# A recommender tower on one core: SBUF laid out anew, with TensorE's operands first and on multiples of 512 bytes

## The reference, cut to what matters

```python
def _cin_layer(X0, Xi, W, b):
    H = W.shape[0]
    F0_, Fi = (X0.shape[1], Xi.shape[1])
    Wr = W.reshape(H, F0_, Fi)
    return jnp.einsum('hjk,bjd,bkd->bhd', Wr, X0, Xi) + b[None, :, None]
...
e = jnp.stack([tbl_0[ids[:, 0]], ..., tbl_38[ids[:, 38]]], axis=1)   # 512 x 39 x 16
for W, b in Ws:                                                       # 3 layers, H = 128
    Xi = _cin_layer(X0, Xi, W, b)
    res.append(Xi.sum(axis=2))
...
h = jnp.concatenate([z, dense_ctx], axis=1)                           # 384 + 16
h = jnp.maximum(h @ W_top1 + b_top1, 0.0)                             # 512
h = jnp.maximum(h @ W_top2 + b_top2, 0.0)                             # 256
y = h @ W_top3                                                        # 1
```

## Time and profile before

| | us |
|---|---|
| median of 3 runs | 668.32 (667.62 to 669.49) |
| the profiled execution, its own time | 667.98 |
| its span, first to last instruction | 666.2 |
| TensorE busy | 644.0 |
| ScalarE, VectorE, GpSimd busy | 480.6, 457.2, 497.3 |

### The profile page before, as it was taken

How to read it: one execution, slowest core, us unless ns; L and a number is a source line. 1 busy time by engine, 2 the same in 40 slices (tenths; PEclk the granted TensorE clock), 3 DMA queues, 4 the chain that set the end, 5 groups by cost and what they waited for, 6 DMA issues and landing times.

```text
span 666.2 us, 11234 instructions
## 1 busy us (share of the span) xinstructions
PE 644.0 (97%) x2676; PEld 478.7 (72%) x2676; DVE 457.2 (69%) x1183; ACT 480.6 (72%) x1737; POOL 497.3 (75%) x467
## 2 busy tenths in 40 slices
PE   3599999999999999999999999999999999999998
PEld 1387677777777777777787777777777777779873
DVE  1467777778686968777725786868687777774820
ACT  1457678878787969697834787878796978784912
POOL 5888888979797988888844797979888885553620
PEclk9989999999999999999999999999999999999999
DMA  6643515151514234142400514132241404002000
GB/s 160 143 107 71 125 25 118 36 121 13 140 15 98 58 68 86 38 115 36 119 11 2 119 13 113 20 78 55 47 85 17 115 10 118 4 4 90 5 1 1
DMA packets 68263, 43.32 MB, mean 65 GB/s; under 512 B 49482, under 2 KB 61709, under 8 KB 66457
## 3 DMA queue, kind: packets, MB, share of 16 engines
q1 hardware_dynamic: 56870, 38.04, 25.1%
q0 software_dynamic: 5184, 1.29, 2.3%
q10 hardware_dynamic: 6158, 3.45, 2.0%
HBM read 39.58 MB, written 1.96 MB: 62 GB/s over the span
## 4 chain that ended last, share of the span: by engine, by line
PE 94%; DMA 3%; SPq 1%; DVE 1%; ACT 1%; issue 1%; POOL 0%; ACTq 0%
PE a_ps L704 40%; PE d_ps L704 25%; PE quad_ps L655 14%; PE g_ps L745 5%; PE quad_ps L758 5%; PE a_ps L871 1%; PE quad_ps L672 1%; DMA rows<-x_first 1%; DMA emb<-tables_dram,rows 1%; PE quad_ps L659 1%; PE d_ps L842 1%; DMA x_first<-emb 1%; DMA picks_sb<-picks_dram 1%; PE rows_ps L842 0%; PE a_ps L842 0%
## 5 line engine op out<-in xcount | busy, mean ns | idle before, releaser
L930 ACT ACTIVATE parts<-a_ps,xt 128x128 f32<-128x128 f32 x1536 | 424.2, 383 | 104.5 <-PE a_ps L704 101.2
L551 DVE SCALAR_TENSOR_TENSOR parts<-d_ps,xt,parts 128x128 f32<-128x128 f32 x704 | 201.8, 343 | 108.2 <-PE d_ps L704 107.8
L311 POOL TENSOR_TENSOR parts<-parts 128x512 f32<-128x512 f32 x128 | 163.8, 1297 | 97.8 <-ACT parts L930 97.0
L704 PE MATMUL a_ps<-w_hi,x_hi 128*128 128x512 f32 x384 | 181.5, 473 | 0.6 <-issue 0.6
L311 POOL TENSOR_TENSOR left<-parts 128x512 f32<-128x512 f32 x128 | 166.8, 1319 | 6.5 <-ACT parts L930 4.9
L285 POOL DMA_INDIRECT emb<-tables_dram,rows_now x150 | 144.6, 964 | 25.2 <-issue 17.9
L704 PE MATMUL a_ps<-w_hi,x_lo 128*128 128x512 f32 x384 | 152.3, 397 | 0.6 <-DVE x_lo L520 0.6
L704 PE MATMUL a_ps<-w_lo,x_hi 128*128 128x512 f32 x384 | 151.5, 395 | 0.0
L704 PE MATMUL d_ps<-w_hi,x_hi 128*128 128x512 f32 (+1 forms) x256 | 127.1, 496 | 0.0
L655 PE MATMUL quad_ps<-products,w_sb 117*128 117x512 f32 (+1 forms) x210 | 107.3, 591 | 0.0
L704 PE MATMUL d_ps<-w_lo,x_hi 128*128 128x512 f32 (+1 forms) x256 | 97.7, 382 | 0.6 <-ACT xt L908 0.6
(11 more groups left out here) (72 smaller groups left out, 426.1 us busy)
## 6 DMA issues: line engine op xcount, KB each, us to landing
shifted<-x_rows SPq DMA_DIRECT2D x45, 312.0 KB
shifted<-x_rows SPq DMA_DIRECT2D x45, 234.0 KB
diag<-xt SPq DMA_DIRECT2D x240, 4.9 KB
rows<-x_rows SPq DMA_DIRECT2D x45, 78.0 KB
emb<-tables_dram,rows_now POOLq DMA_INDIRECT x150, 3.2
w_sb<-w_dram SPq DMA_DIRECT2D x6, 384.0 KB
shifted<-x_first SPq DMA_DIRECT2D x12, 136.5 KB
g_sb<-w_dram ACTq DMA_DIRECT2D x2, 768.0 KB, 9.4
```

The lines of the kernel that those rows point to most:

```text
L311: nc.gpsimd.tensor_tensor(to, parts[:, i % 2, now:now + GF, :], parts[:, i % 2, more:more + GF, :], ALU.add).then_inc(pool_added, 1)
L551: nc.vector.scalar_tensor_tensor(now, d_ps[d % D_RING][:, H * at:H * (at + 1)], xt[:, u, i, j:j + 1], before, ALU.mult, ALU.add).then_inc( ...
L704: return nc.tensor.matmul(bank[:, 0:H * len(fields)], x[:, u, 128 * i:128 * (i + 1)], w[:, fields[0]:fields[-1] + 1, :].rearrange("p j h - ...
L930: last = nc.scalar.activation(parts[:, i % 2, 2 + GF * a + at, :], a_ps[(NA * i + a) % A_RING][:, H * at:H * (at + 1)], ACT.Copy, scale=xt ...
```

## The change

Eleven tensors move to the front of SBUF, behind a new one, `spare`, that nothing uses: `w1_hi`, `w1_lo`, `x1_hi`, `x1_lo`, `w0_sb`, `products`, `w2_sb`, `g_sb`, `x2t`, `diag` and `z`. No size, shape or type changes, and on all five engines the same instructions stand in the same order with the same waits; line numbers below the edit are 3 higher.

```diff
@@ -155,6 +155,20 @@
+        spare = sb("spare", [128, 96])
+        w1_hi = sb("w1_hi", [128, FIELDS, H], F32R)
+        w1_lo = sb("w1_lo", [128, FIELDS, H], F32R)
+        x1_hi = sb("x1_hi", [128, 2, CW], F32R)
+        x1_lo = sb("x1_lo", [128, 2, CW], F32R)
+        w0_sb = sb("w0_sb", [PK, QT, H])
+        products = sb("products", [128, QT, CW])
+        w2_sb = sb("w2_sb", [128, FIELDS, H])
+        g_sb = sb("g_sb", [128, FIELDS, HB])
+        x2t = sb("x2t", [128, 2, H])
+        diag = sb("diag", [128, BLKS, BLK_B, FIELDS + 1])
+        z = sb("z", [128, 3, B])
+
         picks0_sb, picks_sb = sb("picks0_sb", [128, PICKS0], I32), sb("picks_sb", [128, PICKS], I32)
@@ -165,10 +179,6 @@
-        w0_sb = sb("w0_sb", [PK, QT, H])
-        w1_hi = sb("w1_hi", [128, FIELDS, H], F32R)
-        w1_lo = sb("w1_lo", [128, FIELDS, H], F32R)
-        w2_sb = sb("w2_sb", [128, FIELDS, H])
         bias_sb = sb("bias_sb", [128, 3])
@@ -182,18 +192,11 @@
         rows3 = sb("rows3", [PK, CW])
-        products = sb("products", [128, QT, CW])
-        x1_hi = sb("x1_hi", [128, 2, CW], F32R)
-        x1_lo = sb("x1_lo", [128, 2, CW], F32R)
...
-        x2t = sb("x2t", [128, 2, H])
-
-        diag = sb("diag", [128, BLKS, BLK_B, FIELDS + 1])
-        g_sb = sb("g_sb", [128, FIELDS, HB])
-        z = sb("z", [128, 3, B])
```

## The result

The changed kernel takes 663.51 us (median of 6 runs, 661.84 to 664.97) against 668.04 us (6 runs, 666.76 to 669.49). The ratio is 0.9938, with a 95% interval from 0.9924 to 0.9953: 4.5 us or 0.6% faster.

What follows compares the result with a forecast made beforehand. TensorE, busy 644.0 of 666.2 us, was taken to bound the kernel. Every term of the change was taken at 0, so the forecast was no change (666.3 to 670.3 us counted as same), with a range of 661 to 672 us.

Steps and rivals of the forecast that it cites:

- What bounds the kernel: Whole kernel: TensorE, busy 644.0 of 666.2 us, sets the time; other engines wait for it, with about 100 us cushion each.
- The sum of 434.5 us for layer 1: Layer-1 matmuls: 1728 at 0.232 us plus 192 at 0.175 us, meeting the chain's 433 us.
- 1 ns a matmul is 1.9 us: Layer-1 matmuls, all 1920: each ns more per matmul was priced at 1.9 us, 0.3% of the time.
- Moving operands of layer 1: Layer-1 `w1` stream, remainder 64 to 0: taken at 0, bounds -9.6 to +15.4 us.
- The irregular intervals: Layer-1 loop: matmul intervals vary from 0.227 to 0.24 us though nobody waits; the prediction could not say by what.
- B: Rival, layer-1 stream: irregularity goes, intervals settle at 0.227 us, 9.6 us less, 658.7 us; chance 0.12.
- 2 to 6 us: Layer-1 stream: the partial gain called as likely as the full 9.6 us of B.
- Rival A: Layer-1 stream: 19 ns excess is misaligned 512-byte reads; freed, 0.2145 us a matmul, 32.7 us less, 635.6 us; chance 0.05.
- Rival C: Layer-1 matmuls: `w1` stream and `x1` weight load, run in step, collide; +15.4 us, 683.7 us, half as likely; chance 0.09.
- fp32 operands and weight loads at 0: TensorE's fp32 passes (0.429 us) and weight loads (188 to 191 ns): new remainders cost 0; passes at most 2.1 us.
- DMA and the start: First 34 us, `emb0` write and read back into `rows3`: taken at 0, bounds +-1.9 us.
- same: Whole kernel: time within 666.3 to 670.3 us, not told from no change; chance 0.74.

Runs made afterwards that it cites:

- the mixed small kernel: TensorE alone on zeros, repeating one fp32 matmul, then six or nine float32r ones; with nine, 2947 ns all at 0, 2951 to 2954 mostly at difference 128.

## Why the prediction was right or wrong

**What bounds the kernel: right.** The time followed TensorE's own instructions; the other engines moved by about a microsecond. The sum of 434.5 us for layer 1 was right too, and so was "1 ns a matmul is 1.9 us", as an upper bound. One part was not: engines behind TensorE were held to be covered by about 100 us of idle time each. That is a sum over the program. With TensorE 0.36 us a chunk faster, VectorE came late at one place in each of 12 chunks and took 1.0 us back. The prediction listed the waits of TensorE's matmuls and not those of its weight loads, where this bank already stood:

```profile
PEld d_ps L704 <- DVE parts L551: 8.7, 39, 0.2
```

**Moving operands of layer 1, taken at 0: wrong, and the failed step is the comparison.** The term measured 3.4 ns for each matmul of 512 columns. The prediction set `w1` at remainder 64 against `ctx_split` at 448 and found the same 1.10 us. Two things were wrong with it. It compared remainders of the moving operand, where the pair of operands counts: `ctx_split` and its stationary partner in `x1_lo` both start at 448, difference 0, the good case, and `w1` over `x1` is difference 128, the bad one. And it read a lone float32r matmul behind fp32 passes, in which the good case does not show: in the mixed small kernel the interval at that place is 630 to 639 ns at difference 0 and 631 to 638 at 128. A row that does not stand in a run of its own kind cannot price the run.

**The irregular intervals: the right trace, not followed.** The prediction saw 0.227 to 0.24 in a loop where nobody waits and wrote "I can't say by what". Those were the effect. It priced the end of it rightly, 0.227 for each, and overstated the total (9.6 us for B) by taking all 1920; the mean fell by 3.4 ns, not 5, and 1.0 us came back as waits. The measured 4.5 us lie in the "2 to 6 us" that the prediction named as equally likely, without a working of its own; that the result fell inside the stated range is owed to this rider and not to the term of 0.

**Rival A (the full 19 ns as a misaligned read): wrong.** Its 0.2145 us never appears. 226.7 is the lowest settled value for 512 columns. The argument against A, that a limit on bytes explains the growth with length, was no better: above a column a cycle the lowest settled values stand 13.3 ns for 512 columns, 13.3 for 384 and 6.7 for 256, which neither a fixed extra block nor a price for each byte gives. What sets this excess is open. The figure of the Trainium skill that stood beside it (216 ns for N = 512) is not reached by float32r with fresh weights in any case here.

**Rival C: the mechanism half right, its sign wrong.** The moving read and the weight load do depend on each other's start, as C said, and `w1` and `x1` "run in step" after the change, but in step is the best case and not the worst. A difference of 192 shows what the worst pair tried costs this kernel: +0.14% (0.00 to 0.28%), where C had priced 15.4 us, 2.3%. The argument against C, that loads last 188 to 191 ns whatever the partner, proved nothing, since the load's own duration is 188 in the good case as well:

```profile
L707 PEld LDWEIGHTS a_ps<-w_hi,x_hi 128*128 128x128 f32 x384 | 72.3, 188 | 25.8 <-issue 8.5 <-ACT parts L933 0.2
```

The Trainium skill ("SBUF — State Buffer", Who interferes with whom) gives TensorE two independent read ports, and by that the pair of starts should not matter; the measurement decides, and here it does matter, by up to 7 ns in 227.

**fp32 operands and weight loads at 0: right.** 429.2 ns a pass at both layouts, and the kernel before with 128 bytes ahead of `x1_hi`, with all fp32 operands at their old remainders, has the full gain.

**DMA and the start, 0 with +-1.9 us: right as a bound.** The read back into `rows3` took 4.37 us in the changed kernel's chain, where it was 5.82, and 6.03 in the new layout at remainder 64:

```profile
23.90 4.37 DMA rows<-x_first
```

```profile
23.51 6.03 DMA rows<-x_first
```

By the start of the second chunk the changed kernel is 0.85 us ahead in the two profiles, more than a chunk's gain. This can't be put down to the layout: the first chunk takes 47.9 to 52.3 us over the eleven profiles, and 48.5 to 52.3 among those with a difference of 0.

The four profiles with `w1_sb` off a multiple of 256 bytes have 5.09 to 6.03 us (mean 5.70), the seven with it on one 4.37 to 5.41 (mean 4.90). The queue of ScalarE, whose packets are mostly `w1_sb`'s 512-byte rows, took 1.9 to 2.0% of the engines' time there and 1.8% here; from the records a 512-byte packet took 31 to 32 ns against 28.
**The chances.** 0.74 for "same" was too much for a step that I knew to rest on rows from elsewhere, while the loop itself showed an unexplained variation of 13 ns in an operation that is 65% of the time.

## What to carry to other kernels

Where TensorE streams float32r matmuls back to back with a fresh stationary operand each, look at the distance in SBUF between the starts of the two operands modulo 256 bytes: for 512 columns a distance of 0 was 2.5 to 3% better for each matmul in a long run than 128, and one gap of 128 bytes got all of it; for 256 columns another distance was best, so measure it with a stream of the kernel's own shape. In these kernels alignment as such, and where in SBUF a tensor lay, did nothing for TensorE. And when identical instructions show different intervals in a loop in which nobody waits, treat this as a cost to be explained and not as noise. When effects are below 1%, hold one loop pass of two traces against each other: it separated differences of 0.1 us that the times of whole runs blur.

## What the runs showed of the hardware

Float32r matmuls with 128 x 128 weights never ran at a column a cycle: the best settled intervals are 544 cycles at 2.4 GHz for 512 columns, 416 for 384 and 272 for 256, all three multiples of 16, and the same stream can settle in different rhythms (232.5 or 233.3 ns for a difference of 128). A smaller weight load does not help: with 64 and 16 stationary columns at difference 0 a matmul took 230.0 and 231.1 ns, where 128 columns took 226.7. fp32 passes took 429.2 ns at either of the two differences tried, 0 and 128.
